# Where a decoder kernel loads and splits its stages' weights: in each stage, or in the stage in front

## The reference

```python
x = x + attn0(layernorm(x))      # 16 heads of 8, rope, causal, with biases
x = x + mlstm(layernorm(x), ctx, ctx)   # gates from [q,k,v], stabilised exp(D) * qk / sqrt(32), per-head norm
h = layernorm(x)
w = softmax(h @ gW + gb); topv, topi = top_k(w, 3)
x = x + shared(h) + sum_e gated[e] * expert_e(h) + h
# shared: 128 -> 512 -> 128, each of 15 routed experts: 128 -> 256 -> 128, exact GELU, all with biases
x = x + attn1(layernorm(x))      # ALiBi, causal
x = x + cross(ctx, layernorm(x)) # 8 heads of 64; keys and values from both, rope on the context's keys
x = x + soft_moe(x)              # 64 experts x 32 slots, softmax over the batch and over the slots
```

## Time and profile before

| | us |
|---|---|
| three executions | 2108.49, 2109.78, 2114.78 |
| median | 2109.78 |
| profiled execution | 2105.3 |
| span of its trace | 2103.5 |

### The profile page before, as it was taken

One profiled execution on the slowest core, in us unless ns is written; L12 is line 12 of the kernel. 1 busy time (PEld: TensorE's weight loads), 2 busy tenths in 40 slices (PEclk: granted clock), 3 DMA queues, 4 the chain that ended last, 5 costly groups with the idle time before them and its releaser, 6 DMA issues. The chain is left out here.

```text
span 2103.5 us, 62415 instructions
## 1 busy us (share of the span) xinstructions
PE 1865.1 (89%) x23360; PEld 1476.1 (70%) x23422; DVE 1459.6 (69%) x3889; ACT 1447.1 (69%) x4195; POOL 1118.4 (53%) x1445
## 2 busy tenths in 40 slices
PE   5799788399999999699859999867999999999898
PEld 3566556277777777466648888745888888888787
DVE  7699748466666665477746676667777777777567
ACT  5588657388888888488848888746666666666542
POOL 5567437388888889455423333228444444545520
PEclk9999969699999999799989999998999999999999
DMA  3100000432222222000011111120000000000101
GB/s 87 36 25 25 12 8 3 97 91 71 73 72 73 70 73 76 12 2 2 2 42 32 32 32 32 27 69 4 5 15 17 3 18 5 15 15 3 55 8 38
DMA packets 60908, 72.51 MB, mean 34 GB/s; under 512 B 10553, under 2 KB 38985, under 8 KB 60353
## 3 DMA queue, kind: packets, MB, share of 16 engines
q1 hardware_dynamic: 51392, 64.32, 10.4%
q10 hardware_dynamic: 9216, 4.20, 0.7%
HBM read 51.46 MB, written 4.44 MB: 27 GB/s over the span
## 5 line engine op out<-in xcount | busy, mean ns | idle before, releaser
L1037 POOL TENSOR_TENSOR ff_hl<-ff_hid,ff_hh 128x512 fp32r<-128x512 f32 x272 | 351.3, 1307 | 89.4 <-ACT ff_hh L1280 81.8
L1897 POOL TENSOR_TENSOR sm_zsum<-sm_zsum,sm_logits 128x512 f32<-128x512 f32 x120 | 154.6, 1288 | 273.2 <-ACT sm_logits L1923 271.5
L1201 DVE TENSOR_TENSOR ff_hid<-ff_p_b,ff_gates 128x512 f32<-128x512 f32 x240 | 164.8, 687 | 151.9 <-ACT ff_p_b L1269 151.2
L1940 ACT ACTIVATE sm_sT<-sm_p_s 128x512 f32<-128x512 f32 x128 | 69.5, 595 | 219.3 <-PE sm_p_s L1733 219.3
L594 ACT ACTIVATE at_pr<-at_p_s,at_small 128x64 f32<-128x64 f32 x512 | 154.9, 329 | 60.4 <-DVE at_small L480 60.4
L1280 ACT ACTIVATE ff_hh<-ff_hid 128x512 fp32r<-128x512 f32 x272 | 169.9, 625 | 35.5 <-DVE ff_hid L1201 35.5
L1269 ACT ACTIVATE ff_p_b<-ff_p_h,ff_b 128x512 f32<-128x512 f32 x240 | 157.1, 655 | 20.7 <-PE ff_p_h L1100 19.6
L1909 POOL TENSOR_TENSOR sm_logits<-sm_logits,sm_peak 128x512 f32<-128x512 f32 x128 | 163.0, 1295 | 12.5 <-ACT sm_comb L1958 11.9
L1747 PE MATMUL sm_p_l<-g_phi,g_xnT 128*128 128x256 f32 x512 | 142.3, 404 | 26.5 <-ACT sm_logits L1968 25.4
L561 POOL TENSOR_TENSOR at_kblk<-at_kT,at_heads 128x512 f32<-128x512 f32 x128 | 131.7, 1049 | 37.8 <-PE at_p_s L459 26.4
L1098 PE MATMUL ff_p_h<-ff_xh,ff_w1h 128*128 128x512 f32 x272 | 113.8, 418 | 25.2 <-ACT ff_hid L1269 11.5
(11 more groups left out here) (297 smaller groups left out, 5603.2 us busy)
## 6 DMA issues: line engine op xcount, KB each, us to landing
ff_gates<-kept_gates SPq DMA_DIRECT2D x120, 256.0 KB, 3.1
xa_kturn<-xa_ksin SPq DMA_DIRECT2D x128, 64.0 KB, 2.0
at_turned<-at_terms SPq DMA_DIRECT2D x64, 64.0 KB, 1.9
sm_w<-in_w_soft SPq DMA_DIRECT2D x8, 512.0 KB, 3.4
ff_whole<-in_L_ffn_rW SPq DMA_DIRECT2D x30, 128.0 KB, 3.6
early_xs<-in_x ACTq DMA_DIRECT2D x32, 64.0 KB, 1.9
ld_ctx<-in_ctx ACTq DMA_DIRECT2D x32, 64.0 KB, 2.1
x_kept<-early_xs SPq DMA_DIRECT2D x1, 2048.0 KB, 7.4
```

Source lines behind the costliest of these rows:

```text
L1037: eng.tensor_tensor(hl[:, q, :], hid[:, q, :], hh[:, q, :].bitcast(F32), ALU.subtract).then_inc(h_split, 1)
L1201: dve.tensor_tensor(h, p_b[c % 2][:, :], gates[:, n % GR, :], ALU.mult).then_inc(scaled, 1)
L1897: pool.tensor_tensor(z, z, logits[:, j % RING_L, :, :], ALU.add).then_inc(summed, 1)
```

## The change

The weights and tables of each stage move to memory contexts that live longer, and the stage in front issues their loads; a class Ahead counts them. load_and_norm's SP issues attention 0's ten. Attention 0's SP issues one load after the turning DMAs of each of the tiles 4 to 24: the recurrence's eleven and the raw weights of the experts' chunks 0 to 11 (ten). The recurrence's SP issues the experts' five tables, and after the sixth split the raw weights of chunks 12 to 23 (twelve loads). The experts' SP issues the last five experts' loads between its gates and attention 1's five at its end. Attention 1's SP issues the cross attention's five at its start.

In attention, DVE's memset becomes four, one for each slot, behind bvb and bo; only ScalarE's value copies of the first four tiles wait for them. In the recurrence, ScalarE rounds chunks 0 to 11 at its start (six copies of 128x512), DVE subtracts (six), and POOL's sel copy waits for the recurrence's own loads only. In the experts the remaining 22 chunks are rounded and split in six pieces, of four chunks and a last one of two, at chunks 4, 8, 12, 16, 20 and 24 of turn 0. The core of the diff:

```diff
+class Ahead:
+    def __init__(self, m, name):
+        self.arrived, self.issued = m.stack.enter_context(m.nc.semaphore(f"{name}_in")), 0
+    def load(self, sync, loads):
+        for dst, src in loads:
+            sync.dma_start(dst, src).then_inc(self.arrived, 16)
+            self.issued += 16
+    def wait(self, eng):
+        eng.wait_ge(self.arrived, self.issued)
...
+            at["in"].load(sync, at["loads"][0])
...
+    at["loads"] = [[(at[n][:, :], io[f"w{layer}_{n}"]) for n in names] + [(at["bias"][:, :], io[f"c_bias{layer}"])] for layer in range(2)]
...
         @block.sync
         def _(sync):
-            for dst, src in loads:
-                sync.dma_start(dst, src).then_inc(consts_in, 16)
+            if not rope:
+                later.load(sync, later_loads)
             for k in range(NT if rope else 0):
                 sync.wait_ge(rope_terms, 4 * (k + 1))
@@ -360,11 +379,12 @@
                     sync.wait_ge(k_ready, k - 1)
                 for odd in range(2):
                     sync.dma_start(turned[1 - odd:P:2, k % 2, :, :], terms[odd:P:2, k % 3, 1, :, :]).then_inc(rope_turned[k % 2], 16)
+                if k >= 4:
+                    later.load(sync, later_loads[k - 4:k - 3])
         @block.tensor
         def _(pe):
-            pe.wait_ge(consts_in, 16 * len(loads))
-            pe.wait_ge(zeroed, 1)
+            at["in"].wait(pe)
             if rope:
                 pe.wait_ge(bv_spread, 1)
...
         def _(dve):
-            dve.memset(vblk[:, :, :, :, :], 0.0).then_inc(zeroed, 1)
-            dve.wait_ge(consts_in, 16 * len(loads))
+            at["in"].wait(dve)
             if rope:
                 dve.tensor_copy(bvb[:, :], cols[:, 2:3].to_broadcast([P, P])).then_inc(bv_spread, 1)
                 dve.wait_ge(bv_done, 1)
                 dve.tensor_tensor(bo[:, :], p_v[:, 0:D], bo[:, :], ALU.add).then_inc(bo_made, 1)
+            for v in range(R):
+                dve.memset(vblk[:, v, :, :, :], 0.0).then_inc(zeroed, 1)
             def turn(t, u):
                 k, v = t + 1, (u + 1) % R
@@ -539,7 +560,7 @@
...
         def _(act):
-            act.wait_ge(consts_in, 16 * len(loads))
-            act.wait_ge(zeroed, 1)
             def turn(t, u):
                 def turn_copy(k, v, hf):
@@ -612,6 +631,8 @@
                 k, v = t + 2, (u + 2) % R
                 if has(k):
                     act.wait_ge(v_done, k + 1)
+                    if k < R:
+                        act.wait_ge(zeroed, k + 1)
                     if has(k - R):
...
         @block.sync
         def _(sync):
-            for dst, src in gate_loads:
-                sync.dma_start(dst, src).then_inc(gates_in, 16)
-            for dst, src in loads:
-                sync.dma_start(dst, src).then_inc(consts_in, 16)
+            ff["in"].load(sync, ff["loads"])
+            sync.wait_ge(w_split, FIRST // 2)
+            ff["raw_in"].load(sync, routed_loads(ff, io, range((FIRST - CS) // CE, (2 * FIRST - CS) // CE)))
         @block.tensor
...
-            dve.wait_ge(gates_in, 16 * len(gate_loads))
+            ml["in"].wait(dve)
             dve.tensor_copy(wp[:, 0, 0:2 * MH], wg[:, 0, :]).then_inc(gw_summed, 1)
             dve.tensor_tensor(wp[:, 1, 0:2 * MH], wg[:, 1, :], wg[:, 2, :], ALU.add).then_inc(gw_summed, 1)
+            for i, (low, whole, high) in enumerate(first_weights(ff)):
+                dve.wait_ge(w_rounded, i + 1)
+                dve.tensor_tensor(low, whole, high.bitcast(F32), ALU.subtract).then_inc(w_split, 1)
             dve.wait_ge(gates_done, 2)
             dve.tensor_copy(gT[:, 1, :], p_x[:, 0, 1, :]).then_inc(gT_copied[1], 1)
-            dve.wait_ge(consts_in, 16 * len(loads))
             for hf in range(2):
                 dve.wait_ge(gates_turned, hf + 1)
                 for i in range(4):
@@ -864,7 +890,7 @@
         @block.gpsimd
         def _(pool):
-            pool.wait_ge(consts_in, 16 * len(loads))
+            ml["in"].wait(pool)
...
         @block.scalar
         def _(act):
+            ml["in"].wait(act)
+            for low, whole, high in first_weights(ff):
+                act.activation(high, whole, ACT.Copy).then_inc(w_rounded, 1)
             act.wait_ge(gates_done, 1)
             act.activation(gT[:, 0, :], p_x[:, 0, 0, :], ACT.Copy).then_inc(gT_copied[0], 1)
             act.wait_ge(gate_step, 3)
             act.activation(nabs[:, :, :], nabs[:, :, :], ACT.Exp).then_inc(logs, 1)
             act.wait_ge(logs, 1)
             act.activation(expn[:, :, :], nabs[:, :, :], ACT.Ln, bias=1.0).then_inc(logs, 1)
-            act.wait_ge(consts_in, 16 * len(loads))
...
+def routed_loads(ff, io, experts_of):
+    loads = []
+    for e in experts_of:
+        at = slice((CS + CE * e) % FIRST, (CS + CE * e) % FIRST + CE)
+        loads += [(ff["whole"][:, 0, at, :], io["L0_ffn_rW1"][e].rearrange("i (c f) -> i c f", c=CE)),
+                  (ff["whole"][:, 1, at, :], io["L0_ffn_rW2"][e].rearrange("(c f) d -> f c d", c=CE))]
+    return loads
+def experts_weights(m, ff):
+    for n in ("w1h", "w2h", "w1l", "w2l"):
+        ff[n] = m.sb(n, [P, NC_FF, P], F32R)
+def first_weights(ff):
+    parts = []
+    for lo in range(0, FIRST, 4):
+        at = slice(lo, lo + 4)
+        parts += [(ff["w1l"][:, at, :], ff["whole"][:, 0, at, :], ff["w1h"][:, at, :]),
+                  (ff["w2l"][:, at, :], ff["whole"][:, 1, at, :], ff["w2h"][:, at, :])]
+    return parts
...
+    pieces = [slice(lo, min(lo + 4, NC_FF)) for lo in range(FIRST, NC_FF, 4)]
+    last_experts = [range(lo, min(lo + 2, NE)) for lo in range((2 * FIRST - CS) // CE, NE, 2)]
+    LAST_AT = [6, 8, 10]
...
-        def piece_of(c):
-            return [i for i, p in enumerate(pieces) if p.start <= c < p.stop][0]
-        def spread_gates(sync, t, experts_of):
+        def spread_gates(sync, t):
             at = slice(t * N, (t + 1) * N)
-            if experts_of[0] == 0:
-                sync.wait_ge(gT_copied, t + 1)
-                sync.dma_start(gates_d[:, at], gT[0:NE, t % R, :]).then_inc(gates_kept, 16)
-                sync.wait_ge(gates_kept, 16 * (t + 1))
-            for e in experts_of:
+            sync.wait_ge(gT_copied, t + 1)
+            sync.dma_start(gates_d[:, at], gT[0:NE, t % R, :]).then_inc(gates_kept, 16)
+            sync.wait_ge(gates_kept, 16 * (t + 1))
+            for e in range(NE):
+                if t == 0 and e in LAST_AT:
+                    i = LAST_AT.index(e)
+                    sync.wait_ge(w_split, 2 * (i + 1))
+                    for dst, src in routed_loads(ff, io, last_experts[i]):
+                        sync.dma_start(dst, src).then_inc(w_in[i], 16)
                 n = NE * t + e
                 if n >= GR:
                     sync.wait_ge(scaled, CE * (n - GR + 1))
@@ -1054,18 +1099,9 @@
         @block.sync
         def _(sync):
-            for dst, src in loads:
-                sync.dma_start(dst, src).then_inc(consts_in, 16)
-            for i, piece in enumerate(w_loads):
-                if i >= 2:
-                    sync.wait_ge(w_split, 2 * (i - 1))
-                for dst, src in piece:
-                    sync.dma_start(dst, src).then_inc(w_in[i], 16)
-                if i == 1:
-                    spread_gates(sync, 0, range(GR))
-            spread_gates(sync, 0, range(GR, NE))
-            for t in range(1, NGR):
-                spread_gates(sync, t, range(NE))
+            for t in range(NGR):
+                spread_gates(sync, t)
+            at["in"].load(sync, at_loads)
...
-                        if isinstance(t, int) and t == 0:
-                            pe.wait_ge(w_split, 2 * (piece_of(c) + 1))
+                        if t == 0 and c >= FIRST:
+                            pe.wait_ge(w_split, 2 * ((c - FIRST) // 4 + 1))
...
-        FIRST_SPLIT = {-1: [NC_FF - 1], 0: [1, 2, 3, 4]}
-        assert len(pieces) == 5
+        SPLIT_AT = [4, 8, 12, 16, 20, 24]
+        assert len(SPLIT_AT) == len(pieces)
+        def whole_of(i, a):
+            at, n = pieces[i].start % FIRST, pieces[i].stop - pieces[i].start
+            return whole[:, a, at:at + n, :]
         def split_weights(dve, i):
-            at = pieces[i]
-            n = at.stop - at.start
             dve.wait_ge(w_rounded, 2 * (i + 1))
             for a, (low, high) in enumerate(((w1l, w1h), (w2l, w2h))):
-                dve.tensor_tensor(low[:, at, :], whole[:, i % 2, a, 0:n, :], high[:, at, :].bitcast(F32), ALU.subtract).then_inc(w_split, 1)
+                dve.tensor_tensor(low[:, pieces[i], :], whole_of(i, a), high[:, pieces[i], :].bitcast(F32), ALU.subtract).then_inc(w_split, 1)
...
-                    if isinstance(t, int) and t <= 0 and c in FIRST_SPLIT[t]:
-                        split_weights(dve, FIRST_SPLIT[t].index(c) + (1 if t == 0 else 0))
+                    if t == 0 and c in SPLIT_AT:
+                        split_weights(dve, SPLIT_AT.index(c))
...
-            act.wait_ge(consts_in, 16 * len(loads))
```

(41 more changed lines are left out.)

126 lines of the change are left out of this document (59 added, 67 removed).

## The result

| | before | changed |
|---|---|---|
| executions beside each other, first chip | 2106.35 to 2114.78, median 2109.14 | 2079.52 to 2085.51, median 2084.30 |
| the same on a second chip | 13, median 2112.24 | 4, median 2085.02 |
| profiled execution | 2105.3 | 2085.5 |
| span of its trace | 2103.5 | 2083.6 |

The ratio is 0.9866 (95% interval 0.9851 to 0.9881) on the first chip and 0.9872 (0.9854 to 0.9890) on the second. By the medians the change is worth 25 to 27 us, by the ratios 28 and 27 (intervals 25 to 31 and 23 to 31), where 31.2 was forecast. 2084.3 is inside the range of 2069 to 2091.

What follows compares the result with a forecast made beforehand. TensorE, with work for 89% of the span, was taken as the bound, with load waits at stage starts removable: 4.2 + 1.0 + 17.2 + 3.65 + 5.2 = 31.2 us off the 2109.8 median, 2078.6 us, range 2069 to 2091.

Steps and rivals of the forecast that it cites:

- The cross attention: Start of the cross attention: without its load wait, the first matmul comes 5.2 us earlier (4.3 to 5.9), one collision included.
- Attention 1: Start of attention 1: load wait gone, memset no longer beside loads, first DVE step 3.65 us earlier (3.3 to 4).
- Attention 0: Start of attention 0: wait for ten loads gone, memset now bare, first rope term 4.2 us earlier (3.9 to 4.5).
- a term that I had at 0 to 1: load_and_norm: issuing attention 0's ten loads there costs 0, at most 1 us if they delay the first input tile.
- Recurrence, head: Recurrence's start: gate-weight wait gone but POOL's copy may delay DVE's sum, gain 1.0 us (0 to 2.1); splits cost 0.
- Experts: Experts' head and turn 0: no waits for tables or raw weights, gain 17.2 us together (11 to 22).
- the 8.8 beyond TensorE's own pace: Experts' turn 0: ScalarE's groups, table loads and next tile's copies, less TensorE's lead, add 8.8 us; turn 1 starts at 452.4.
- The mis-sized term: Experts' turn 0: one collision of DVE's splits with POOL, 1.08 us, in each group of four chunks, making it 6.6 us.
- Case 5: Recurrence and turn 0: TensorE's clock stays at 1.2 GHz throughout, making the kernel slower, 2142 us; chance 0.03.
- The prediction's own sign of being wrong: Recurrence: a granted clock of 0.50 after 310 us, one of several signs that would show the prediction wrong.
- Case 3: Experts' turn 0: both splits of each piece wait for a whole POOL instruction, groups 8.4 us, total 2087.6; chance 0.18.
- Case 2: Turn 0, recurrence, cross attention: the port shared by DVE and POOL costs nothing, groups 5.5 us, total 2071.3; chance 0.20.

Runs made afterwards that it cites:

- exp_own: Changed kernel with the experts' block again loading, rounding and splitting its own tables and weights, none of it in the recurrence's head; 2102.39 us.
- pieces6: Changed kernel with the last 22 chunks rounded and split in four pieces of six (last of four) instead of six of four; 2084.27 us.
- warm2: Changed kernel with additional matmuls, results unused, in TensorE's gaps in the recurrence's head and the experts' turn 0; 2067.86 us.
- the pair with the gaps filled: Changed kernel and kernel before, both with the same unused matmuls in TensorE's gaps in recurrence and experts; 2067.86 and 2101.21 us.
- late_split: Changed kernel with the first twelve chunks' rounding and splitting moved from the recurrence's head to the experts' start, twelve raw loads behind; 2084.62 us.

## Why the prediction was right, point by point

- **Starts.** The cross attention (5.2 forecast, 5.3 measured) was right with its mechanism: DVE's second split meets POOL's subtraction and takes 1.22 us instead of 0.68.

```profile
1053.50 0.98 POOL L1558 TENSOR_TENSOR xa_zl<-xa_z,xa_zh 128x256 fp32r<-128x256 f32 x1
...
1053.82 1.22 DVE L1489 TENSOR_TENSOR xa_wvl<-xw_wv,xa_wvh 128x512 fp32r<-128x512 f32 x1
```

  Attention 1 (3.65, 3.8) was right in that the memset is uncovered, but its number is in part luck: the four memsets take 0.5 us more than the one, and they start 0.5 us sooner behind the experts' last instruction (0.77 us after its start instead of 1.25). Attention 0 was 0.5 under: there the 0.5 of the memsets shows, and load_and_norm ended later, a term that I had at 0 to 1.
- **Recurrence, head.** 1.0 forecast, 1.2 measured, for the reason given. POOL's copy of sel holds DVE's first copy, of one input, for 1.53 us, and not only the sum behind it:

```profile
256.97 1.89 POOL L895 COPY ml_sel<-mw_hot 128x2048 f32<-128x2048 f32 x1 [1.59 <-POOLq L65]
...
257.35 1.53 DVE L808 COPY ml_wp<-mw_wg 128x8 f32<-128x8 f32 x1
```

  The six roundings and splits were done at 262.56, DVE's copy of the gates stood at 264.33, and exp_own's head is as late without them: hidden, as said.
- **Experts.** 17.2 forecast, 16.7 and 16.3 measured. The first expert matmul was due 8.31 after the memset (396.94 - 388.63) and came 8.34 after it. From there to turn 1's logits 58.2 was forecast, 58.6 and 59.1 measured. So the 8.8 beyond TensorE's own pace were right as a sum, but they are made up differently. The mis-sized term is the meeting of splits with POOL: one per group of 1.08 us was assumed, 1.2 us in all was measured, and pieces6 shows that fewer splits gain nothing. Nor did the sum have the second low stretch, 6.8 us behind the Exp's gap; warm2, at 2.4 GHz all through its turn 0, took 57.4, so the low clock was worth 1.2 to 1.7 us there. ScalarE was busy for 52.0 of the 58.6 us and waited 2.7 for DVE, so the pace of turn 0 is mostly ScalarE's own work, as the sum had it; how the rest is made up was not taken apart, and the sum's 1.0 for the next tile's copies has no row either. That the total fits is luck in part.
- **Between the stages.** The step that failed is the silent one: that all stretches between the starts keep their length. In the traces they gave back 10.8 and 8.4 us, in the medians 4 to 6 and in the ratios 3 and 4, which the intervals (up to 31) hardly tell from nothing. In the first trace 3.6 are in the recurrence, and the pair with the gaps filled shows that these are the granted clock. Case 5 had named it, but as all or nothing, with 3 in 100; a part of it, 41 us or more instead of 27, came in six of eight traces of the changed kernel and the variants that kept the second tile's gap. The prediction's own sign of being wrong, a granted clock of 0.50 after 310 us, was just reached: the clock rose at 310.1 in the first trace and at 315.4 in late_split. Whether the change makes the long stretch more frequent is open, since the kernel before has one trace without additional matmuls. Attention 1 took about 0.5 to 2.0 us longer in all variants but one and the cross attention mostly 1.5 to 3, of which up to 0.8 and 2.4 also lie between traces of the kernel before with and without additional matmuls; for these no experiment gives the cause, nor for the 3.5 to 4.0 in the last stage, in which executions of either kernel differ as much.
- **Rivals.** Case 3, the exclusive lock at full price, would have given 2087.6, and the measured 2084.3 is nearer to that (3.3) than to the forecast (5.7). Its mechanism is refuted all the same: not both splits of each piece waited, but three of twelve in all. By the Trainium skill, "SBUF — State Buffer", section "Who interferes with whom", it is who starts first that blocks the other; in this trace nine of DVE's twelve splits found the ports free or had them first. Case 2 had the price of turn 0's splits nearly right (1.2 us where it had 0), but not that turn 0 gets no shorter by it, and in the recurrence and the cross attention the collisions that it left out came.

## What to carry to other kernels

Where each stage waits for its own loads, read the idle time in the bracket of the stage's first instructions. The gains can be added up: the five starts gave 30.7 and 29.6 us in two traces, where 31.2 was forecast. The whole kernel kept 25 to 28 of them. Then look at what stood in the shadow of the load, like a memset, and at which idle engine can take it. And look at the granted clock behind each gap of TensorE before and after a change: filling six gaps of 0.5 to 5 us with matmuls that nobody reads was worth 15 to 17 us to the changed kernel here and 9 to the kernel before, beside the 25 to 28 of the whole change. And compare more than one trace: the profiled execution before was 4 to 7 us under its kernel's medians, and that alone is of the size of what was sought between the stages.

## What the runs showed of the hardware

- TensorE was busy without a gap for over 27 us (283 to 310 in the first trace, 296 matmuls) at a granted clock of 0.50. What it ran are small matmuls, nearly all in fp32, most of them over 32 or 64 rows and 64, 65 or 128 columns. Being busy did not bring the clock back for so long, while in warm2 the same work kept it at 1.00 once it had it.
- The same program has low stretches of 27.3 and of 41.0 us there in two executions, and the same gap of 3.08 us is followed by a low stretch in the changed kernel and not in late_split.
- POOL's instruction of 1.3 us can hold a DVE instruction of 0.22 us on 128x60 for 0.7 us, and beside its copy of 1.89 us one of DVE on 128x8, 0.17 us before, took 1.4 longer.
